# A decoder layer on one core: the causal mask of all scores added by VectorE while it takes the maxima, in place of mask products on TensorE

## The chip, the cores and the metric

The kernel runs as one program on one core of a Trainium2 chip. The metric is the device time of one execution in microseconds, lower is better; of several executions the median counts. The engines are named as in the profile: PE is TensorE (PEld its weight loads), DVE VectorE, ACT ScalarE, POOL GpSimd, SP the engine that only issues DMAs.

## What is computed

A decoder layer for 16 sequences of 256 tokens of 512 features, in float32: causal self attention with rotary positions, cross attention over a context, and a mixture of eight experts. Only self attention bears on the change:

```python
q = (x @ wq).reshape(b, s, N_HEADS, HEAD_DIM).transpose(0, 2, 1, 3)     # 32 heads of 16
k = (x @ wk).reshape(b, s, N_KV_HEADS, HEAD_DIM).transpose(0, 2, 1, 3)  # 8, each for 4 heads
...
scores = jnp.einsum('bhqd,bhkd->bhqk', q, k) / HEAD_DIM ** 0.5
causal = jnp.tril(jnp.ones((s, s), dtype=bool))
scores = jnp.where(causal[None, None], scores, -jnp.inf)
probs = jax.nn.softmax(scores, axis=-1)
out = jnp.einsum('bhqk,bhkd->bhqd', probs, v)
```

The softmax subtracts each row's maximum, which is to be taken over the keys up to the query only.

## The kernel before

The stages run one after the other: constants and weights, projections (`stage_qkv`), `stage_attention`, `stage_cross`, `stage_experts`. The change is in `stage_attention`, in one constant, and in the mask's tile.

Attention works in 32 halves: a half is one sequence with 16 of its 32 heads (four groups of keys, each with four query heads). Scores are computed twice. First, with queries as rows, only to find the maxima (`score`, L750 to L762, and the reductions at L654). The negated maxima go into `nb`, are transposed (`turn_m`), copied, and moved by DMA into a 49th row of the queries `qs`. Two halves later the scores are computed again with keys as rows and the maximum subtracted by that 49th row (`shifted`, L764), ScalarE takes the exponential (L592), GpSimd zeroes what lies above the diagonal (L500), and TensorE multiplies by the values (`values`, L774). This second way is not touched.

A half has 12 pieces of the first kind, s0 to s11, in six pairs p = 0 to 5; the two pieces r = 0, 1 of a pair lie in the two halves of the array's rows and are issued in turns. Each piece fills one PSUM bank of 128 x 512: for p = 0, 1 (first 128 queries) four heads of 128 keys, for p = 2 to 5 (last 128 queries) two heads of 256 keys. The first products overwrite the bank. Then one product for each piece, the bf16 identity times the mask (zero up to the diagonal, -1e30 above), is added onto the blocks on the diagonal: 512 columns for p = 0, 1, and 256 for p = 2 to 5. Its end gives the semaphore `scores`. VectorE waits for it and reduces the whole bank in one instruction to 4 or 2 negated maxima.

The banks are a ring of four (`ring`). 18 results pass through it in a half in the order of `TURNS`: s0, s1, m (the maxima turned), qa, s2, s3, s4, s5, qb, qc, s6, s7, s8, s9, qd, k, s10, s11, where qa to qd and k are transposes of the next half's queries and keys, which ScalarE (qa, qb, qd) and VectorE (qc at L630, k at L635) copy out. `taken` makes TensorE wait until the result four turns earlier has been read: so s2 and s3 wait for the maxima of s0 and s1, s6 for s4, s10 for s8. `score` takes both banks before the first product of a pair.

The order on each engine is written out by hand. TensorE, for each p of `step`: `shifted` of the half two before, `score`, then at p = 0 the maxima turned and qa, at p = 1, 3, 5 a product with values, at p = 2 qb and qc, at p = 4 qd and k. VectorE, for each p: the two pieces, then qc at p = 2, k at p = 4, and once in two halves a reciprocal at p = 5.

Outside attention, `stage_constants` lets GpSimd set the mask (L149, L161) while the weights are loaded.

Of the kernel before, what the change touches and what calls it, by code (L numbers as in the profile page):

```python
# [13 lines left out]
BF16 = mybir.dt.bfloat16  # L14
# [21 lines left out]
ST = SLOTS // P  # L36
EPS = 1e-5
MASKED = -1e30
ONE = 1
CH = 4  # L40

# [7 lines left out]
def wait_apart(eng, sem, value, passed, start=ONE):  # L49

    if not (isinstance(value, int) and value <= 0):
        eng.wait_ge(sem, start + value).then_inc(passed, 1)
# [54 lines left out]
def stage_constants(nc, io, t):  # L107


    with Scope(nc) as s:  # L110
# [34 lines left out]
        @block.gpsimd  # L145
        def _(pool):
            pool.memset(t["ident"][:], 0.0).then_inc(ident_set, 1)
            pool.memset(t["identb"][:], 0.0).then_inc(ident_set, 1)
            pool.memset(t["mask"][:], 0.0).then_inc(mask_set, 1)  # L149
            pool.memset(t["ones"][:], 1.0)  # L150
            pool.memset(t["upper"][:], 1.0).then_inc(mask_set, 1)
            pool.memset(t["avg"][:], 1.0 / P)
            pool.memset(t["half"][:], -0.5)
            pool.memset(t["eps"][:], EPS)
            pool.wait_ge(ident_set, ONE + 2)
            for m in (t["ident"], t["identb"]):
                pool.affine_select(out=m[:], in_=m[:], compare_op=ALU.not_equal, fill=1.0, base=0,
                                   pattern=[[-1, P]], channel_multiplier=1)
            pool.wait_ge(mask_set, ONE + 2)

            pool.affine_select(out=t["mask"][:], in_=t["mask"][:], compare_op=ALU.is_ge, fill=MASKED, base=0,  # L161
                               pattern=[[-1, P]], channel_multiplier=1)

            pool.affine_select(out=t["upper"][:], in_=t["upper"][:], compare_op=ALU.is_gt, fill=0.0, base=0,
                               pattern=[[1, P]], channel_multiplier=-1)
# [203 lines left out]
def stage_attention(nc, io, t):  # L369
# [6 lines left out]
    with Scope(nc) as s:  # L376
# [43 lines left out]
        def bank(e, name):  # L420

            return ring[(2 * e + TURNS.index(name)) % 4]
# [203 lines left out]
        def _(dve):  # L626
# [19 lines left out]
            def step(j, w, q, e):  # L646
                h = 2 * j + e
                for p in range(6):
                    if within(h, 0, HALVES):
                        for r in range(2):  # L650
                            n = 2 * p + r
                            heads, qb = (slice(0, REP), 0) if p < 2 else (slice(p // 2 * 2 - 2, p // 2 * 2), 1)
                            dve.wait_ge(sm["scores"], ONE + PIECES * h + n + 1)
                            dve.tensor_reduce(nb[e][:, r, p % 2, heads, qb],  # L654
                                              bank(e, f"s{n}")[:].rearrange("p (h k) -> p h k", h=heads.stop - heads.start),
                                              AX.X, ALU.max, negate=True).then_inc(sm["maxima"], 1)
                    if p == 2 and within(h + 1, 0, HALVES):
                        keep_q(h + 1, (2 * q + e + 1) % 4, bank(e, "qc"))
                    if p == 4 and within(h + 1, 0, HALVES):
                        keep_k(h + 1, (2 * q + e + 1) % 4, bank(e, "k"))  # L660
                    if e == 1 and p == 5 and within(j - 2, 0, B):
                        dve.wait_ge(sm["den_loaded"], ONE + 16 * (j - 2) + 16)
                        wait_apart(dve, sm["rec_stored"], 16 * (j - 2), passed_dve)
                        dve.reciprocal(rec[:], den[:]).then_inc(sm["den_turned"], 1)
                    if p == 5 and isinstance(h, int) and h == HALVES + 1:
                        first_splits()
# [36 lines left out]
        def _(pe):  # L703
# [45 lines left out]
            def score(j, q, e, p):  # L749
                i = 2 * q + e  # L750
                width = P if p < 2 else S
                heads = range(REP) if p < 2 else range(p // 2 * 2 - 2, p // 2 * 2)
                banks = [taken(2 * j + e, e, f"s{2 * p + r}")[:].rearrange("p (h k) -> p h k", k=width) for r in range(2)]
                for c, n in enumerate(heads):
                    for r in range(2):
                        rows = slice(64 * r, 64 * r + 48)
                        pe.matmul(banks[r][:, c, :], qs[i][rows, p % 2, n, width - P:width],
                                  ks[i][rows, p % 2, 0:width], start=True, stop=False, skip_group_check=True)
                for r in range(2):
                    pe.matmul(banks[r][:, :, width - P:width], t["identb"][:],  # L760
                              t["mask"][:].unsqueeze(1).to_broadcast([P, len(heads), P]), start=False, stop=True,
                              skip_group_check=True).then_inc(sm["scores"], 1)  # L762

            def shifted(h, i, p):  # L764
                kb, qb = BLOCKS[p // 2]
# [1025 lines left out]
def decoder_layer(nc, io):  # L1791
    with Scope(nc) as s:
        t = {}
        t["ident"] = s.sb("ident", [P, P])
        t["identb"] = s.sb("identb", [P, P], BF16)
        t["mask"] = s.sb("mask", [P, P], BF16)
        t["ones"] = s.sb("ones", [P, P])
        t["upper"] = s.sb("upper", [P, P])
        t["avg"] = s.sb("avg", [P, P])
# [106 lines left out]
```

## Time and profile before

| | us |
|---|---|
| median of 3 runs | 2931.71 |
| the runs | 2930.7 to 2936.34 |
| the profiled execution | 2930.81 |
| its span, first to last instruction | 2929.1 |
| PE busy | 2793.4 (95%) |
| DVE busy | 1236.7 (42%) |
| ACT busy | 877.9 (30%) |
| POOL busy | 838.8 (29%) |
| mean granted clock of TensorE, as a share of full | 0.982 |

The page divides the span into 40 slices of 73 us. Attention lies in the slices from 188 to 600 us, where DVE is busy for about seven tenths; the experts, from about 1090 us, are two thirds of the span, and the chain that ended last lies nearly all in them. As the stages follow each other, what attention gains or loses moves the end by as much. A busy time is the sum of the recorded durations; instructions that overlap are pipelined, so it is the starts of consecutive instructions that tell what one costs.

### The profile page before, as it was taken

To read this page: it belongs to the slowest core of one execution; us is meant where nothing else is said; L and a number is where in the kernel's file an instruction comes from. 1 tells how busy PE (TensorE), PEld (TensorE's weight loads), DVE (VectorE), ACT (ScalarE), POOL (GpSimd) and SP (SyncE) were. 2 spreads that over 40 slices of the span, in tenths; PEclk is the share of its full clock that TensorE was granted. 3 is DMA by queue.
4 is the path that set the end of the run, shared out by engine and by line. 5 is a ranking of instruction groups with operands and counts; after the bars stand their busy time and mean duration, and the time that the engine had idled before them with its cause. 6 is when DMAs were issued, how large, how long until landed. Compare 5 with 4: busy or idle time off the path is not lost.

```text
span 2929.1 us, 45881 instructions
## 1 busy us (share of the span) xinstructions
PE 2793.4 (95%) x16150; PEld 2283.9 (78%) x16150; DVE 1236.7 (42%) x2152; ACT 877.9 (30%) x1697; POOL 838.8 (29%) x1306
## 2 busy tenths in 40 slices
PE   6989999988999939999999999999999999999998
PEld 6865555556666529999999999999999999999997
DVE  6756777747888833332232232132133133133111
ACT  1126666641555512221121121122122122122110
POOL 4546776631166641101101111011021021011010
PEclk9999999999999969999999999999999999999999
DMA  3101222242122223221122032032033033022010
GB/s 109 43 1 31 48 45 48 55 92 87 68 84 75 77 83 106 91 86 64 51 92 75 26 108 83 15 109 87 12 108 101 11 100 104 14 90 85 26 47 21
DMA packets 97078, 194.68 MB, mean 66 GB/s; under 512 B 22126, under 2 KB 23758, under 8 KB 96800
## 3 DMA queue, kind: packets, MB, share of 16 engines
q1 hardware_dynamic: 75072, 131.77, 15.1%
q0 software_dynamic: 21856, 60.73, 6.6%
q8 instruction: 116, 1.90, 0.3%
q14 instruction: 34, 0.28, 0.0%
HBM read 148.77 MB, written 38.94 MB: 64 GB/s over the span
## 4 chain that ended last, share of the span: by engine, by line
PE 62%; DMA 0%; POOL 0%; DVE 0%; issue 0%; ACT 0%; DVEq 0%; POOLq 0%
PE ex_hid L1775 31%; PE ex_acc L102 10%; PE ex_acc L103 10%; PE ex_acc L104 10%; PE ex_xb L1745 1%; DMA ex_ys<-xn_dram,ex_slot_gather 0%; POOL out_dram L1627 0%; POOL ex_ys L1607 0%; DVE ex_ys L1688 0%; POOL ex_xg L1592 0%; DMA ex_ys<-slot_table_dram 0%; PE ex_acc L1745 0%; DVE ex_h0l L1696 0%; ACT ex_h0h L1655 0%; DVE ex_xT0l L1671 0%
## 5 line engine op out<-in xcount | busy, mean ns | idle before, releaser
L1696 DVE SCALAR_TENSOR_TENSOR ex_h0l<-ex_hid,ex_h0h 128x640 fp32r<-128x640 f32 x128 | 105.5, 824 | 682.8 <-ACT ex_h0h L1655 682.8
L1696 DVE SCALAR_TENSOR_TENSOR ex_h1l<-ex_hid,ex_h1h 128x640 fp32r<-128x640 f32 x128 | 105.4, 824 | 602.9 <-ACT ex_h1h L1655 602.3
L1655 ACT ACTIVATE ex_h0h<-ex_hid 128x640 fp32r<-128x640 f32 x128 | 90.1, 704 | 734.5 <-PE ex_hid L1775 734.5
L1655 ACT ACTIVATE ex_h1h<-ex_hid 128x640 fp32r<-128x640 f32 x128 | 90.1, 704 | 729.8 <-PE ex_hid L1775 729.8
L654 DVE TENSOR_REDUCE at_nb<-at_ring 128x2 f32<-128x512 f32 (+1 forms) x384 | 246.8, 685 | 121.1 <-PE at_ring L760 120.9
L1597 POOL COPY ex_gi<-ex_slot_gather 128x1 int32 (+1 forms) x82 | 15.3, 187 | 918.2 <-PE ex_xb L1745 913.3
L102 PE MATMUL ex_acc<-ex_w_h,ex_h1h 128*128 128x512 f32 x640 | 254.8, 398 | 0.0
L102 PE MATMUL ex_acc<-ex_w_h,ex_h0h 128*128 128x512 f32 x640 | 253.4, 396 | 0.0
L103 PE MATMUL ex_acc<-ex_w_l,ex_h0h 128*128 128x512 f32 x640 | 250.3, 391 | 0.0
L103 PE MATMUL ex_acc<-ex_w_l,ex_h1h 128*128 128x512 f32 x640 | 250.2, 391 | 0.0
L104 PE MATMUL ex_acc<-ex_w_h,ex_h1l 128*128 128x512 f32 x640 | 249.8, 390 | 0.0
L104 PE MATMUL ex_acc<-ex_w_h,ex_h0l 128*128 128x512 f32 x640 | 249.5, 390 | 0.0
L592 ACT ACTIVATE at_pT<-at_st 128x512 f32<-128x512 f32 x384 | 210.4, 609 | 124.1 <-PE at_st L770 124.1
L1775 PE MATMUL ex_hid<-ex_xT0h,ex_w_h 128*128 128x320 f32 x1024 | 234.3, 310 | 3.4 <-DVE ex_xT0l L1671 1.4
L1775 PE MATMUL ex_hid<-ex_xT0h,ex_w_l 128*128 128x320 f32 x1024 | 234.2, 310 | 0.0
L1775 PE MATMUL ex_hid<-ex_xT0l,ex_w_h 128*128 128x320 f32 x1024 | 234.1, 310 | 0.0
L1775 PE MATMUL ex_hid<-ex_xT1h,ex_w_l 128*128 128x320 f32 x1024 | 233.4, 309 | 0.0
L1775 PE MATMUL ex_hid<-ex_xT1l,ex_w_h 128*128 128x320 f32 x1024 | 233.3, 309 | 0.0
L1775 PE MATMUL ex_hid<-ex_xT1h,ex_w_h 128*128 128x320 f32 x1024 | 232.7, 308 | 0.0
L1627 POOL DMA_INDIRECT out_dram<-ex_ys,ex_rows_out x80 | 80.7, 1009 | 519.5 <-DVE ex_ys L1688 504.9
L1775 PEld LDWEIGHTS ex_hid<-ex_xT0h,ex_w_h 128*128 128x128 f32 x1024 | 176.7, 189 | 15.4 <-issue 4.1
L1775 PEld LDWEIGHTS ex_hid<-ex_xT1h,ex_w_h 128*128 128x128 f32 x1024 | 176.4, 188 | 10.0
(273 smaller groups left out, 5665.2 us busy)
## 6 DMA issues: line engine op xcount, KB each, us to landing
ex_raw<-in_w_tiles_dram SPq DMA_DIRECT2D x256, 256.0 KB, 2.8
x_in<-in_x_dram SPq DMA_DIRECT2D x32, 256.0 KB, 2.7
act<-at_raw SPq DMA_DIRECT2D x128, 64.0 KB
at_recb<-o_rec_dram SPq DMA_DIRECT2D x16, 512.0 KB
k<-in_x_dram SPq DMA_DIRECT2D x32, 256.0 KB, 2.7
cx_ctx<-in_ctx_dram SPq DMA_DIRECT2D x16, 512.0 KB, 3.8
out_dram<-cx_res SPq DMA_DIRECT2D x16, 512.0 KB, 2.8
xn_dram<-cx_prob SPq DMA_DIRECT2D x16, 512.0 KB, 2.8
```

The source lines that it names most:

```text
L102: eng.matmul(out, lhs[0], rhs[0], start=first, stop=False, **kw)
L103: eng.matmul(out, lhs[0], rhs[1], start=False, stop=False, **kw)
L104: return eng.matmul(out, lhs[1], rhs[0], start=False, stop=last, **kw)
L592: act.activation(pT[slot][:], st[n % 3][:], ACT.Exp).then_inc(sm["probs"], 1)
L654: dve.tensor_reduce(nb[e][:, r, p % 2, heads, qb], bank(e, f"s{n}")[:].rearrange("p (h k) -> p h k", h=heads.stop - heads.start), AX.X, AL ...
L1597: pool.tensor_copy(gi[r][:], slot_gather[:, bass.ds(n, 1)]).then_inc(sm["idx_col"], 1)
L1627: pool.indirect_dma_start(io["out_rows"][:, :], bass.IndirectOffsetOnAxis(rows_out[:, i:i + 1], 0), ys[:, i, :], None, bounds_check=B * S ...
L1655: act.activation(h[f % 2][0][:], hid[:, :, 0:HB], ACT.Relu).then_inc(sm["h_hi"], 1)
L1696: dve.scalar_tensor_tensor(h[f % 2][1][:], hid[:, :, 0:HB], 0.0, f32(h[f % 2][0][:]), ALU.max, ALU.subtract).then_inc(sm["h_lo"], 1)
L1745: q = pe.transpose(bank[:, k * P:(k + 1) * P], source[:, k * P:(k + 1) * P], t["ident"][:])
L1775: i = pe.matmul(hid[:, z, 0:HB], w1[a][:, f, k, :], xT[b][q][:, k, z * HB:(z + 1) * HB], start=k == 0 and a + q == 0, stop=k == KD - 1 and ...
```

## The change

The products with the mask are taken out, and the last score product of a piece gives the semaphore. The mask's tile is 256 columns wide, the first 128 of them zero, so that it fits a head of 256 keys; the last 128 fit a head of 128. VectorE takes a piece head by head: an operation adds the mask to the head's scores, multiplies by -1, writes the result back over the scores, and puts the smallest of the results, which is the negated maximum, into `nb`. Its wait is an instruction of its own.

```diff
+LARGEST = 3e38
...
-            pool.affine_select(out=t["mask"][:], in_=t["mask"][:], compare_op=ALU.is_ge, fill=MASKED, base=0,
+            pool.affine_select(out=t["mask"][:, P:S], in_=t["mask"][:, P:S], compare_op=ALU.is_ge, fill=MASKED, base=0,
                                pattern=[[-1, P]], channel_multiplier=1)
...
                             n = 2 * p + r
-                            heads, qb = (slice(0, REP), 0) if p < 2 else (slice(p // 2 * 2 - 2, p // 2 * 2), 1)
-                            dve.wait_ge(sm["scores"], ONE + PIECES * h + n + 1)
-                            dve.tensor_reduce(nb[e][:, r, p % 2, heads, qb],
-                                              bank(e, f"s{n}")[:].rearrange("p (h k) -> p h k", h=heads.stop - heads.start),
-                                              AX.X, ALU.max, negate=True).then_inc(sm["maxima"], 1)
+                            x = bank(e, f"s{n}")
+                            wait_apart(dve, sm["scores"], PIECES * h + n + 1, passed_dve)
+                            width, qb, heads = (P, 0, range(REP)) if p < 2 else (S, 1, range(p // 2 * 2 - 2, p // 2 * 2))
+                            for c, a in enumerate(heads):
+                                y = x[:, c * width:c * width + width]
+                                m = dve.tensor_tensor_reduce(y, y,
+                                                             t["mask"][:, S - width:S], -1.0, LARGEST, ALU.add, ALU.min,
+                                                             nb[e][:, r, p % 2, a, qb:qb + 1])
+                            m.then_inc(sm["maxima"], 1)
...
-                        pe.matmul(banks[r][:, c, :], qs[i][rows, p % 2, n, width - P:width],
-                                  ks[i][rows, p % 2, 0:width], start=True, stop=False, skip_group_check=True)
-                for r in range(2):
-                    pe.matmul(banks[r][:, :, width - P:width], t["identb"][:],
-                              t["mask"][:].unsqueeze(1).to_broadcast([P, len(heads), P]), start=False, stop=True,
-                              skip_group_check=True).then_inc(sm["scores"], 1)
+                        m = pe.matmul(banks[r][:, c, :], qs[i][rows, p % 2, n, width - P:width],
+                                      ks[i][rows, p % 2, 0:width], start=True, stop=True, skip_group_check=True)
+                        if c == len(heads) - 1:
+                            m.then_inc(sm["scores"], 1)
...
-        t["mask"] = s.sb("mask", [P, P], BF16)
+        t["mask"] = s.sb("mask", [P, S], BF16)
```

## Rows read from the trace of the kernel before

**Rows 1.** Windows: stretch, then busy us (x instructions) by engine, granted clock, DMA.
```profile
400.00:450.00 50.00, 49.24 (x394) 26.99 (x390) 35.22 (x57) 34.09 (x70) 36.92 (x54) 1.00 0.21 43
```
**Rows 2.** Waits from 250 to 550 us: who waited for whom, total us, times, longest.
```profile
DVE at_nb L654 <- PE at_ring L760: 87.8, 139, 1.2
...
PEld at_ring L757 <- DVE at_nb L654: 25.7, 70, 0.6
```
**Rows 3.** Timeline, PE: start, us, line, operation, out<-in, count [idle before].
```profile
456.84 0.60 PE L760 MATMUL at_ring<-mask,identb 128*128 128x512 bf16 x2
457.28 0.27 PE L746 MATMUL at_ring<-ident,at_nb 128*32 128x128 f32 x1
...
458.61 0.66 PE L757 MATMUL at_ring<-at_ks,at_qs 48*128 48x128 f32 x8 [0.19 <-DVE at_nb L654]
459.20 0.60 PE L760 MATMUL at_ring<-mask,identb 128*128 128x512 bf16 x2
459.74 1.07 PE L784 MATMUL at_pv<-at_pT,at_vc 128*32 128x512 f32 x8
460.74 0.50 PE L770 MATMUL at_st<-at_qs,at_ks 49*128 49x512 f32 x2
461.07 0.40 PE L757 MATMUL at_ring<-at_ks,at_qs 48*128 48x256 f32 x4
461.41 0.39 PE L760 MATMUL at_ring<-mask,identb 128*128 128x256 bf16 x2
461.64 1.04 PE L727 MATMUL at_ring<-ident,at_qst 128*128 128x128 f32 x8
```
**Rows 4.** Timeline of the same half on DVE.
```profile
457.27 1.29 DVE L654 TENSOR_REDUCE at_nb<-at_ring 128x4 f32<-128x512 f32 x2 [0.96 <-PE at_ring L760]
459.63 1.29 DVE L654 TENSOR_REDUCE at_nb<-at_ring 128x4 f32<-128x512 f32 x2 [1.07 <-PE at_ring L760]
461.73 1.29 DVE L654 TENSOR_REDUCE at_nb<-at_ring 128x2 f32<-128x512 f32 x2 [0.81 <-PE at_ring L760]
...
463.83 1.29 DVE L654 TENSOR_REDUCE at_nb<-at_ring 128x2 f32<-128x512 f32 x2 [0.22 <-PE at_ring L760]
465.82 1.29 DVE L654 TENSOR_REDUCE at_nb<-at_ring 128x2 f32<-128x512 f32 x2 [0.70 <-PE at_ring L760]
...
469.12 0.54 DVE L664 RECIPROCAL at_rec<-at_den 128x64 f32<-128x64 f32 x1
470.17 1.29 DVE L654 TENSOR_REDUCE at_nb<-at_ring 128x4 f32<-128x512 f32 x2 [0.50 <-PE at_ring L760]
```
**Rows 5.** Timeline, DVE: the first maxima of halves 0, 3 and 31.
```profile
189.43 1.29 DVE L654 TENSOR_REDUCE at_nb<-at_ring 128x4 f32<-128x512 f32 x2 [1.23 <-PE at_ring L760]
...
224.20 1.29 DVE L654 TENSOR_REDUCE at_nb<-at_ring 128x4 f32<-128x512 f32 x2 [0.96 <-PE at_ring L760]
...
587.66 1.29 DVE L654 TENSOR_REDUCE at_nb<-at_ring 128x4 f32<-128x512 f32 x2 [0.97 <-PE at_ring L760]
```
**Rows 6.** Timeline, DVE in cross attention: 512 and 1024 columns.
```profile
1003.90 0.69 DVE L1214 TENSOR_REDUCE cx_nmx<-cx_bank 128x1 f32<-128x512 f32 x1
1004.51 1.22 DVE L1233 TENSOR_TENSOR cx_res<-cx_ctx,act 128x1024 f32<-128x1024 f32 x1
```
**Rows 7.** Timeline, ACT in cross attention: operations with an accumulator output.
```profile
1004.83 0.68 ACT L1135 ACTIVATE cx_prob<-cx_bank,cx_nmx 128x512 f32<-128x512 f32 x1
1005.40 0.20 ACT L1135 ACTIVATION_READ_ACCUMULATOR cx_prob<-cx_bank,cx_nmx 128x1 f32 x1
1005.49 0.69 ACT L1135 ACTIVATE cx_prob<-cx_bank,cx_nmx 128x512 f32<-128x512 f32 x1
```
**Rows 8.** Timeline, DVE in cross attention: two tiny instructions in a row.
```profile
1009.67 0.25 DVE L1315 BATCH_NORM_AGGREGATE cx_mv<-cx_st 128x2 f32<-128x6 f32 x2
```
**Rows 9.** Timeline, DVE behind attention: the second has a wait instruction ahead of it.
```profile
652.19 0.68 DVE L670 TENSOR_TENSOR at_qs<-act,at_qs 128x512 fp32r<-128x512 f32 x1
...
652.79 0.69 DVE L682 BATCH_NORM_STATS2 op_st<-act 128x6 f32 x1
```

## The prediction

> **What bounds the kernel now.** I read the slices of the page first. Attention (0.19 to 0.60 ms of the span) is the only stage the change touches; before it lie the projections, behind it cross attention and the experts, whose instructions stay as they are. The stretch 400 to 450 us [rows 1] shows TensorE busy for 49.2 of 50 us at the full clock, VectorE for 35.2. A busy TensorE is not TensorE at its peak, so I went on to the waits [rows 2]: from 250 to 550 us VectorE waits 87.8 us for the mask products, and TensorE's weight loads of the scores wait 25.7 us for the maxima. The two pass the four ring banks back and forth. Then I laid one half (12 pieces) of TensorE [rows 3] beside the same half of VectorE [rows 4]. The half begins at 457.27 and the next at 470.17: 12.90 us. The first maxima of half 3 start at 224.20 and of half 31 at 587.66 [rows 5], so the mean of 28 halves is 12.98 us.
>
> In that half two things alternate. After s0 and s1, TensorE has to wait for both banks (s2 and s3 take the banks of s0 and s1): VectorE ends at 458.56, the eight products of s2 and s3 start at 458.61, their masks at 459.20, and VectorE starts again at 459.63, idle for 1.07 us. From there to s8 TensorE's own list is the later one: values 1.00 us (459.74 to 460.74), shifted scores 0.33 (to 461.07), scores 0.34, masks 0.23 (to 461.64), transposes. VectorE waits 0.81, 0.22 and 0.70 us for it. So both matter, TensorE more.
>
> **What the change takes away.** A half has two pairs of mask products of 512 columns, 0.44 us a pair (456.84 to 457.28), and four of 256 columns, 0.23 us a pair (461.41 to 461.64) [rows 3]: 2 x 0.44 + 4 x 0.23 = 1.80 us, in 32 halves 57.6 us of TensorE. That is the most it could give, and only if nobody else becomes late. It also shortens every answer to VectorE by one mask product: the maxima can start when the last score is out.
>
> **What it adds on VectorE.** Now a piece is one reduction over 512 columns; two in a row last 1.29 us, one of them 0.685, so the pitch is 0.605 us [rows 4]. The slope of a column comes from 1024 columns in 1.22 us against 512 in 0.69 [rows 6]: 1.04 ns. Of the 0.605 us, 0.532 are columns and 0.073 is the fixed part of an instruction. After the change pieces 0 to 3 are four operations over 128 columns each, pieces 4 to 11 two over 256: the columns stay the same, the fixed part is paid 32 times a half, not 12 times. One operation is 0.133 + 0.073 = 0.206 us, or 0.266 + 0.073 = 0.339 us.
>
> These operations also put out an accumulator, and no VectorE row does that. The nearest rows are ScalarE's [rows 7]: its exponential with a sum is an ACTIVATE and, 0.57 us later, a row of its own, ACTIVATION_READ_ACCUMULATOR, after which the next ACTIVATE starts 0.09 us later. I expect the same pair on VectorE. The price of the read is bounded below by nothing (the read lies wholly beside the next operation) and above by two amounts: the read waits until the main operation is through (its full 0.152 us of latency, 0.685 - 0.533, not 0.073) and then takes its own slot. Between them stands the pitch of two tiny VectorE instructions, 0.25 us for two of 0.165, so 0.085 us [rows 8]; ScalarE's 0.09 agrees. I take 0.085: a pair costs 0.291 us (128) or 0.424 us (256). A piece then costs 1.16 us (0 to 3) or 0.85 us (4 to 11) in place of 0.605. VectorE's work of a half grows from 14 x 0.605 + 0.22 (half a reciprocal) = 8.7 us to 4 x 1.16 + 8 x 0.85 + 2 x 0.605 + 0.22 = 12.9 us, by itself as long as the half is now.
>
> The Trainium skill, "Vector Engine (DVE) Microarchitecture Reference", section 5.2, gives about 75 ns of fixed cost per instruction, and "VectorE: DVE Perf Modes", section "Two Vector instructions with no wait between them", says that an operation with an accumulator output is two instructions. The trace agrees with the first (0.073 and 0.085) and shows the second for ScalarE alone. By 75 ns for each of the two a half would be 0.3 us shorter than mine and the whole some 8 us faster. Against this change speaks a rule of "VectorE: DVE Perf Modes", section "Rules for kernel authors": it is the number of VectorE operations that is to be kept small, not that of semaphores.
>
> Two smaller costs. Each piece now waits in an instruction of its own. Where the signal is there already that costs nothing: 652.19 to 652.79 is a plain 0.60 us over such a wait [rows 9]. Where VectorE really waits (three times a half), I put 0.05 us, between 0 and 0.1; only the next maxima are queued behind it, and TensorE waits for those. Writing the scores back in place (PSUM to PSUM) has no row either; I take it at nothing, since the write goes beside the reading, and its upper end is half the rate. The larger mask is set once by GpSimd while the projections' weights are still loading, with 180 us to go before its first use; at nothing.
>
> **The half afterwards, laid out in time** (us from the first maxima of the half). s0, s1: 8 x 0.291 = 2.33. Then TensorE must wait for both banks: 0.08 until the last result is out, 0.05 to TensorE, 0.66 for eight score products, 0.05 back, 0.05 for the wait: 3.22. s2, s3 to 5.55. Meanwhile TensorE does values, shifted, s4 and s5 (1.00 + 0.33 + 0.5) and is ready at about 4.9. s4, s5: 4 x 0.424 to 7.25. One copy of queries to 7.85. s6 and s7 need the bank of s5: TensorE from 7.38, out 7.88, VectorE from 7.98 to 9.68. For s8 TensorE is ready at 9.60 (7.82 + 1.00 + 0.33 + 0.45), so on to 11.38. The keys' copy to 11.98, s10 and s11 from 12.11 to 13.81. The next s0 is ready at 14.00; every other half the reciprocal (0.45) ends later, at 14.26. Mean 14.13 us against 12.98: TensorE's list has fallen behind VectorE's everywhere but at the bank waits, and its 1.80 us lie idle.
>
> **The sum.** 28 halves x 1.15 = 32.2 us. The first three halves have little or no value work beside them; now they take 224.20 - 189.43 = 34.8 us [rows 5], then 3 x 13.86 = 41.6: 6.8 more. The last, without copies, goes from 12.2 to about 13.7: 1.5 more. Together 40.5 us. The profiled run took 2930.81 us (span 2929.1), 0.9 under the median of 2931.71, so nothing is to be corrected: 2930.8 + 40.5 = 2971 us, 1.4% slower.
>
> **Rivals.**
> The accumulator's read costs nothing, or is no instruction (faster). Pairs cost 0.206 and 0.339 us, a piece 0.82 or 0.68. VectorE's work is 10.1 us, s2 starts at 2.5, and from there TensorE's list without masks decides: s4 4.2, s6 6.2, s8 7.9, s10 10.0, next s0 11.8. That is 1.18 us less a half: 28 x 1.18 and about 1 more, 2897 us. For it: the waits on the mask products [rows 2] go. Against it: the ScalarE rows. Between 11.8 at no cost and 14.13 at 85 ns, the break-even of 12.98 lies at a read of 43 ns. Chance 0.14.
> The read lands near that point, gain and loss cancel, 2931 +- 6 us. Chance 0.05.
> The read waits for the end of the main operation: 0.418 + 0.085 = 0.503 and 0.370 us a pair, 32 x 0.079 = 2.5 us a half more, of which 0.1 falls into idle time: 32 x 2.4 = 77 us on top, 3048 us. For it: a result must be complete before it is read. Against: ScalarE's read starts 0.12 us before its ACTIVATE's recorded end (0.68 long, read after 0.57). Chance 0.15.
> In-place PSUM traffic halves the rate: 16 x 0.266 + 16 x 0.133 = 6.4 us a half, 3175 us; nothing in the trace for or against. Chance 0.04.
> TensorE, idle in more places, is granted the lower of its two clocks in attention (1.2 instead of 2.4 GHz): its 9.6 us of a half (values 3 x 1.00, transposes 5 x 0.44 + 0.11, shifted 6 x 0.33, scores 4 x 0.33 + 2 x 0.49, from [rows 3]) double and the half is about 19 us, 3165 us. The row of 400 to 450 shows 1.00 although the engine waits inside it, and the gaps that come are under 1.5 us. Chance 0.02.
>
> **How the numbers follow.** The forecast, a VectorE-bound half of 13.4 to 15.0 us, has 0.60 and by itself 2945 to 3005 us (read at 60 to 120 ns, waits 0 to 0.1). Adding the case of no change (down to 2925) and that of the late read (up to 3055) leaves 0.20 out: range 2925 to 3055. A measurement of this kernel tells about 0.2%, 6 us, from no change. Faster 0.14; within 0.2% 0.05; slower 0.60 + 0.15 + 0.04 + 0.02 = 0.81.
>
> **What the profile after would show.** Attention some 40 us longer, everything behind it moved and nothing else changed. VectorE's share in 400 to 450 us from 35 to about 46 of 50 us. 1024 rows of the new operation with 1024 reads of the accumulator, main rows about 0.42 and 0.28 us long, starts 0.42 and 0.29 us apart. VectorE's idle time almost all before s2; TensorE's weight loads of scores waiting for the maxima for well over 100 us in all. No mask products, granted clock 1.00. The forecast is wrong if no read rows appear, if their pitch is far from 0.085, or if the pitch of the main operation isn't that of its columns.

## The result and the profile after

The changed kernel takes 2993.81 us in the median of 4 runs (2989.59 to 2998.31), the kernel before 2932.74; the ratio of the runs is 1.0207, interval 1.0194 to 1.022. It is 61 us slower. The forecast was 2971 us, 40 slower, in a range of 2925 to 3055: the sign and the range were right, the size was short by 21 us. The profiled execution took 2998.31 us (span 2996.6, against 2929.1 before: 67.5 more).

The page of the changed kernel: the busy times, and the clock granted to TensorE in 40 slices of 75 us.

```profile
PE 2793.0 (93%) x15766; PEld 2288.9 (76%) x15766; DVE 1329.6 (44%) x3816; ACT 879.1 (29%) x1697; POOL 844.8 (28%) x1306
...
PEclk9979888888999997999999999999999999999999
...
q14 instruction: 62, 0.51, 0.1%
```

Two things stand in it that the prediction did not have. The clock is at eight tenths in the slices 5 to 10 (300 to 749 us) and at seven in the third, where the kernel before has nine tenths or more in each; and TensorE is busy for 2793 us as before (2793.4), although 57.6 us of products are gone: the rest runs slower. One of the two queues that bring instructions (q14) moved 62 packets in place of 34.

The stretch that answers to [rows 1] (busy us and instructions of PE, PEld, DVE, ACT, POOL, then granted clock), and the waits that answer to [rows 2]:

```profile
400.00:450.00 50.00, 43.83 (x327) 24.10 (x327) 43.39 (x234) 32.78 (x67) 32.10 (x47) 0.93 0.19 36
450.00:500.00 50.00, 41.17 (x276) 22.70 (x274) 37.55 (x210) 28.06 (x58) 27.48 (x42) 0.83 0.20 42
```
```profile
PEld at_ring L762 <- DVE at_nb L658: 64.4, 52, 5.0
PE at_ring L762 <- DVE at_nb L658: 48.4, 49, 4.7
...
DVE at_ring L658 <- PE at_ring L762: 43.6, 81, 1.4
...
DVE at_ring L658 <- issue: 13.2, 8, 2.2
```

TensorE now waits longer for the maxima, 64.4 us at its weight loads where it was 25.7 (the second row is for the most part the same waits, seen at the products), and VectorE half as long for TensorE (43.6 where it was 87.8). The last row is new: VectorE stood still 8 times, 1.2 to 2.2 us each, for nothing that the profile shows. The groups of operations from 250 to 550 us (count, busy us, mean ns):

```profile
L658 DVE CUSTOM_DVE_ANT_0 at_ring<-at_ring,mask 128x256 f32<-128x256 f32 x320 | 126.7, 458 | 21.2 <-PE at_ring L762 20.5
L658 DVE DVE_READ_ACCUMULATOR2_ANT at_nb<- 128x1 f32 x643 | 91.5, 142 | 0.0
L658 DVE CUSTOM_DVE_ANT_0 at_ring<-at_ring,mask 128x128 f32<-128x128 f32 x323 | 82.5, 327 | 36.4 <-PE at_ring L762 23.2 <-issue 13.2
```

The accumulator's read is a row of its own, one for each operation. What it costs is told by the starts. VectorE's timeline (start, duration):

```profile
440.41 0.34 DVE L658 CUSTOM_DVE_ANT_0 at_ring<-at_ring,mask 128x128 f32<-128x128 f32 x1
440.66 0.14 DVE L658 DVE_READ_ACCUMULATOR2_ANT at_nb<- 128x1 f32 x1
440.66 0.34 DVE L658 CUSTOM_DVE_ANT_0 at_ring<-at_ring,mask 128x128 f32<-128x128 f32 x1
...
442.29 0.47 DVE L658 CUSTOM_DVE_ANT_0 at_ring<-at_ring,mask 128x256 f32<-128x256 f32 x1
442.67 0.15 DVE L658 DVE_READ_ACCUMULATOR2_ANT at_nb<- 128x1 f32 x1
442.67 0.47 DVE L658 CUSTOM_DVE_ANT_0 at_ring<-at_ring,mask 128x256 f32<-128x256 f32 x1
```

Operations over 128 columns start 0.25 us apart, those over 256 0.38. The read is recorded over the start of the next operation, so adding its 142 ns to the others would count it twice. From 440.16 to 441.90 lie seven steps, from 441.90 to 443.43 four, so the pitches are 249 and 382 ns: 43 ns over the 206 and 339 that the prediction gave the main operation, half of the 85 it gave the read.

Now a turn of VectorE's loop. Attention has a rolled loop of five bodies of four halves, so four turns; this is the third, VectorE and then TensorE:

```profile
449.86 0.55 DVE L669 RECIPROCAL at_rec<-at_den 128x64 f32<-128x64 f32 x1
452.52 0.30 DVE L658 CUSTOM_DVE_ANT_0 at_ring<-at_ring,mask 128x128 f32<-128x128 f32 x1 [2.11 <-issue]
...
454.79 0.30 DVE L658 CUSTOM_DVE_ANT_0 at_ring<-at_ring,mask 128x128 f32<-128x128 f32 x1 [1.17 <-issue]
```
```profile
450.82 0.49 PE L773 MATMUL at_st<-at_qs,at_ks 49*128 49x512 f32 x2
455.95 1.12 PE L762 MATMUL at_ring<-at_ks,at_qs 48*128 48x128 f32 x8 [4.64 <-DVE at_nb L658]
457.00 1.93 PE L787 MATMUL at_pv<-at_pT,at_vc 128*32 128x512 f32 x8
```

VectorE stops for 2.11 and 1.17 us, TensorE therefore idles for 4.64 us, and then does its eight products with the values in 1.93 us, where they took 1.07 [rows 3]: its clock has fallen to the lower level (granted 0.50 from 456 to 462 us). The other turns look the same (2.15 and 1.14 us, 2.14 and 1.16, 2.08 and 1.27).

### The profile page after: what moved, and what is told of

Read it like the earlier page. It is cut to its first block, busy times and chain, and to the rows that moved or that the text cites. A ratio compares the mean times of both kernels' runs of the same rounds, so it can differ in the third digit from the quotient of the medians.

```text
span 2996.6 us, 47161 instructions
## 1 busy us (share of the span) xinstructions
PE 2793.0 (93%) x15766; PEld 2288.9 (76%) x15766; DVE 1329.6 (44%) x3816; ACT 879.1 (29%) x1697; POOL 844.8 (28%) x1306
## 4 chain that ended last, share of the span: by engine, by line
PE 61%; DMA 0%; POOL 0%; issue 0%; DVE 0%; DVEq 0%; ACT 0%; POOLq 0%
PE ex_hid L1778 30%; PE ex_acc L104 10%; PE ex_acc L103 10%; PE ex_acc L105 10%; PE ex_xb L1748 1%; DMA ex_ys<-xn_dram,ex_slot_gather 0%; POOL out_dram L1630 0%; POOL ex_ys L1610 0%; DVE ex_ys L1691 0%; POOL ex_xg L1595 0%; DMA ex_ys<-slot_table_dram 0%; PE ex_acc L1748 0%; DVE ex_xT0l L1674 0%; DVEq L73 0%; ACT ex_xT0h L1641 0%
## 5 line engine op out<-in xcount | busy, mean ns | idle before, releaser
L658 DVE CUSTOM_DVE_ANT_0 at_ring<-at_ring,mask 128x256 f32<-128x256 f32 (+1 forms) x1024 | 331.8, 393 | 92.9 <-PE at_ring L762 78.6
L501 POOL TENSOR_SCALAR_AFFINE_SELECT at_pT<-at_pT 128x512 f32<-128x512 f32 x256 | 154.9, 635 | 112.1 <-ACT at_pT L593 112.1
```

The source lines that it names most:

```text
L501: pool.affine_select(out=x[:], in_=x[:], compare_op=ALU.is_ge, fill=0.0, base=0, pattern=[[0, REP], [1, P]], channel_multiplier=-1).then_i ...
L658: m = dve.tensor_tensor_reduce(y, y, t["mask"][:, S - width:S], -1.0, LARGEST, ALU.add, ALU.min, nb[e][:, r, p % 2, a, qb:qb + 1])
```

## The experiments

Each kernel's time is given against the kernel before on the same chip. A half is measured from one copy of keys on VectorE to the next; undisturbed means at full clock and away from a turn. It is 12.90 us before and 13.24 to 13.50 us in the changed kernel.

**e1_after_unrolled: the changed kernel with VectorE's loop written out.**

```diff
+        def steps(eng, first, step, unroll=False):
...
+                for j in range(19):
+                    for e in range(2):
+                        step(j, j // 2, j % 2, e)
...
-            steps(dve, first, step)
+            steps(dve, first, step, unroll=True)
```

> The changed kernel, but VectorE's 38 half steps of attention are written out one by one, where five turns of a loop covered 20 of them. In the changed kernel's trace VectorE stands still for 2.1 and 1.15 us, with no releaser, at each of the four points where that loop turns, TensorE then waits 4.6 us, and its granted clock falls. Theory A (three causes: VectorE's longer work, some 0.5 us a half, 16 us; the loop's turns, because the body has become about 380 instructions long; the clock that falls after the gaps): the eight stops vanish, the clock rises in part, 2970 us, 2960 to 2980. Rival B (the stops belong to the new operation, not to the loop): they stay in place and the time stays at 2990 to 2998 us.

Measured: 2971.17 us (2965.17 to 2980.21) against 2929.21, ratio 1.0152 (1.0126 to 1.0177), so +42 where the changed kernel has +61. All eight stops named "issue" are gone. What is left at full clock is this start of s2, TensorE and VectorE:

```profile
521.00 0.50 PE L778 MATMUL at_st<-at_qs,at_ks 49*128 49x512 f32 x2
522.63 0.66 PE L767 MATMUL at_ring<-at_ks,at_qs 48*128 48x128 f32 x8 [1.13 <-DVE at_nb L663]
```
```profile
523.48 0.30 DVE L663 CUSTOM_DVE_ANT_0 at_ring<-at_ring,mask 128x128 f32<-128x128 f32 x1 [0.90 <-PE at_ring L767]
```

The products end at 523.29, the maxima start at 523.48. In two of four 50 us stretches from 350 to 550 us the clock is still 0.90 (e9 and the three runs behind it take that up).

**e2_before_long_body: the kernel before, with 256 waits that are satisfied already, spread over VectorE's loop body.** Its body has then about as many instructions as the changed one (some 378; before, some 122).

```diff
+            def fill(h, p):
+                if not isinstance(h, int):
+                    for _ in range(6 if p % 3 == 0 else 5):
+                        wait_apart(dve, sm["filled"], 5, passed_dve)
...
+                            fill(h, p)
```

> The kernel before, with 256 waits that are long fulfilled put behind the reductions in VectorE's loop body, so that the body has as many instructions as in the changed kernel (about 380); no operation of the change is in it. Theory A: VectorE stands still for 2 to 3 us at the four turns of the loop, and the time rises by 12 us for these and more where the clock falls: 2945 to 2965 us. Rival B: no stops, at most a few us for the waits themselves: 2931 to 2938 us.

Measured: 2955.31 us (2954.62 to 2956.73), ratio 1.009 (1.0073 to 1.0107), +26. The same stops come at the same four places, 2.54, 2.78, 2.46 and 2.47 us:

```profile
315.08 0.55 DVE L670 RECIPROCAL at_rec<-at_den 128x64 f32<-128x64 f32 x1 [0.19 <-issue]
318.17 1.48 DVE L659 TENSOR_REDUCE at_nb<-at_ring 128x4 f32<-128x512 f32 x2 [2.54 <-issue]
```

About 17 of the 26 us lie in the four halves with a stop (16.73 to 18.35 us each, against 13.14 beside them). The satisfied waits cost a little by themselves: the other 16 halves of the loop take 13.12 to 13.27 us and not 12.90, some 4 us in all.

**e13_before_unrolled: the kernel before, written out in the same way.**

> The kernel before, with the loop over pairs of heads written out instead of rolled, and nothing else. Theory A (a loop body that is too long for what VectorE keeps is what pays at a turn, and before's body is short enough): nothing changes, 2928 to 2935 us. The rival (unrolling gains by itself, so that the 22 us that it gave the changed kernel say nothing of the change): 2920 us or less.

Measured: 2931.37 us (2929.87 to 2933.6, 10 runs) against 2932.0, ratio 0.9999 (0.999 to 1.0009). So it is not the loop that costs but its length: a body of some 122 instructions turns for nothing, one of some 378 stops. The instruction queue's packets go the same way (34 before, 56 in e2, 62 after, 51 in e1). The Trainium skill, "Advanced Engine Details and Errata", section "ISA Cache", says that an engine other than TensorE keeps two lines of 256 instructions; the runs agree in so far as a body of 378 pays and one of 122 doesn't, and none lies between. By that size two lines hold 512 instructions, so it doesn't say by itself that 378 must pay. That it is the fetching of the body's start that stops VectorE is inferred from this and the packets; the profile only says "issue".

**e3_dve_part_alone and e4_pe_part_alone: the two parts apart.** e3 has VectorE's new operations and keeps the mask products; e4 has no mask products and keeps the reduction of a whole bank, so its maxima run over all keys of a piece.

```diff
-                for r in range(2):
-                    pe.matmul(banks[r][:, :, width - P:width], t["identb"][:],
-                              t["mask"][:].unsqueeze(1).to_broadcast([P, len(heads), P]), start=False, stop=True,
-                              skip_group_check=True).then_inc(sm["scores"], 1)
```

> VectorE's part alone: maxima head by head with the mask added as in the changed kernel, and TensorE's mask products kept (the mask is added twice, which changes nothing). TensorE has 1.8 us more work a half than in the changed kernel, and VectorE waits one mask product longer at the bank waits. Theory A (TensorE's clock falls because it has too little to do): the clock comes back to near 1.00, and with more work the kernel is faster than the changed one: about 2975 us. Rival C (the clock has little to do with it; the halves are as long as VectorE makes them): slower than the changed kernel by 5 to 15 us: 3000 to 3010 us.

Measured: 3037.86 us (3034.11 to 3038.55), ratio 1.0366 (1.0349 to 1.0383), +109: slower than either theory had it. An undisturbed half is 14.86 us, 1.5 to 1.6 more than in the changed kernel. VectorE's timeline shows why (from s2 on, the last number the idle time before):

```profile
302.79 0.30 DVE L658 CUSTOM_DVE_ANT_0 at_ring<-at_ring,mask 128x128 f32<-128x128 f32 x1 [1.23 <-PE at_ring L765]
307.50 0.43 DVE L658 CUSTOM_DVE_ANT_0 at_ring<-at_ring,mask 128x256 f32<-128x256 f32 x1 [0.42 <-PE at_ring L765]
309.49 0.43 DVE L658 CUSTOM_DVE_ANT_0 at_ring<-at_ring,mask 128x256 f32<-128x256 f32 x1 [0.35 <-PE at_ring L765]
312.08 0.43 DVE L658 CUSTOM_DVE_ANT_0 at_ring<-at_ring,mask 128x256 f32<-128x256 f32 x1 [0.42 <-PE at_ring L765]
```

With VectorE the later engine, each bank goes back late, and every way back carries a mask product. So taking them away is worth 44 to 48 us beside the slow VectorE as well (3038 to 2994), and the prediction's "its 1.80 us lie idle" was wrong.

> TensorE's part alone: no mask products, and VectorE takes the maxima with one reduction a piece as before, now over all keys, masked ones too. This leaves the mask of the maxima out; the softmax is the same for any subtracted value that keeps the exponentials in range. Laid out in time as in the prediction a half is about 11.1 us against 12.98: 1.9 us less, 60 us in all, 2872 us, as long as the clock stays at 1.00. If the clock falls here too (theory D: every relief of TensorE is paid back by its clock) 2900 us or more. If the mask products were hidden anyway: 2925 us or more.

Measured: 2876.17 us (2873.16 to 2878.02), ratio 0.9817 (0.9801 to 0.9833): 53 us faster than the kernel before, 114 faster than the changed one (-53 against +61). From 250 to 550 us a half is 10.94 to 11.23 us, the clock full:

```profile
400.00:450.00 50.00, 48.53 (x411) 27.36 (x410) 41.09 (x66) 39.53 (x83) 42.98 (x66) 1.00 0.26 52
```
```profile
446.16 1.29 DVE L654 TENSOR_REDUCE at_nb<-at_ring 128x4 f32<-128x512 f32 x2 [0.54 <-PE at_ring L757]
448.20 1.29 DVE L654 TENSOR_REDUCE at_nb<-at_ring 128x4 f32<-128x512 f32 x2 [0.75 <-PE at_ring L757]
...
457.13 1.29 DVE L654 TENSOR_REDUCE at_nb<-at_ring 128x4 f32<-128x512 f32 x2
```

This is the best kernel of the study, and it computes the same result: a softmax is the same whatever is subtracted, as long as the exponentials stay in range, and what lies above the diagonal is zeroed behind the exponential anyway. What it gives up is that range: were a masked score far above all the others of its row, they would vanish. With this case's inputs they don't. The two parts nearly add up: +109 - 53 = +56 against +61 measured together, a difference within the intervals.

**e9_plain_wait: e1 with the wait carried by the first operation of a piece.**

```diff
-                            wait_apart(dve, sm["scores"], PIECES * h + n + 1, passed_dve)
+                            dve.wait_ge(sm["scores"], ONE + PIECES * h + n + 1)
```

> As e1, but the wait for the scores is carried by the operation, as in the kernel before, not by an instruction of its own. If that instruction delays each blocked start by 0.15 us (theory W): the starts come 0.04 us after the score products' end, at four to five such places a half 0.5 us less, 2971 - 16 = 2955 us. If the new operation starts late by itself (theory O): 0.19 us as before and 2971 us.

Measured: 2969.65 us (2967.47 to 2971.74), ratio 1.0128 (1.0111 to 1.0145), +38 against +42: nearly no change. But the undisturbed half did fall, to 12.78 to 12.91 us. TensorE and VectorE at the start of s2:

```profile
442.58 0.50 PE L778 MATMUL at_st<-at_qs,at_ks 49*128 49x512 f32 x2
444.22 0.66 PE L767 MATMUL at_ring<-at_ks,at_qs 48*128 48x128 f32 x8 [1.13 <-DVE at_nb L663]
444.81 1.93 PE L792 MATMUL at_pv<-at_pT,at_vc 128*32 128x512 f32 x8
```
```profile
444.91 0.30 DVE L663 CUSTOM_DVE_ANT_0 at_ring<-at_ring,mask 128x128 f32<-128x128 f32 x1 [0.75 <-PE at_ring L767]
```

The maxima start 0.69 us after the products do; in e1 it was 0.85. The 0.16 us are the wait's. In this very half the clock falls: the values take 1.93 us (granted 0.50 from 445 us), with no turn near. The granted clock of the eight stretches from 200 to 600 us is 0.67 0.78 0.94 0.90 0.90 0.90 0.86 0.97 (e1: 0.72 0.93 1.00 0.90 1.00 0.90 0.99 1.00). What the wait gave, more falls of the clock took.

**e5_more_shifted_work, e16_still_more_work, e15_plain_wait_more_work: more products where TensorE waits.** If it is idle time that lets the clock fall, useless work in it must make the kernel faster. The shifted products, which overwrite their bank and so can be repeated, stand just before the waits for the banks.

```diff
-                    pe.matmul(st[n % 3][:], ks[i][rows, p % 2, kb * P:kb * P + P],
-                              qs[i][rows, p % 2, :, qb * P:qb * P + P], start=True, stop=True)\
-                        .then_inc(sm["shifted"], 1)
+                    for _ in range({1: 4, 3: 2, 5: 2}.get(p, 1)):
+                        m = pe.matmul(st[n % 3][:], ks[i][rows, p % 2, kb * P:kb * P + P],
+                                      qs[i][rows, p % 2, :, qb * P:qb * P + P], start=True, stop=True)
+                    m.then_inc(sm["shifted"], 1)
```

e5 is e1 with each of p = 1, 3, 5 twice; e16 is e1 with 4, 3, 3 times; e15 is e9 with 4, 2, 2 times (the diff).

> The changed kernel with VectorE's steps written out (as e1), and TensorE's shifted-score products of p = 1, 3 and 5 issued twice, the second over the first with the same result. They stand right in front of the bank waits, where TensorE idles 0.45 to 1.1 us, and take 0.33 us a pair. So they should lie in idle time and only make TensorE's gaps shorter. Theory A (TensorE's clock falls for want of work, and the halves in which it falls are 0.5 to 2 us longer): the clock stays higher than in e1 in attention, and the kernel with more work is as fast or faster, 2958 to 2968 us against e1's 2971. Rival (the long halves have another cause): 2971 us or up to 5 us more, with the same long halves.

> The unrolled kernel with its own waiting instruction, with the shifted products of the first part given four times and those of the second and third three times. Theory A (work in TensorE's gaps holds its clock): fewer stretches below 1.00 than with each doubled, undisturbed halves still of 13.24 us, and 2952 to 2960 us. The rival (the doubled products had done all that such work can): 2963 us or more.

> The unrolled kernel with the wait carried by the operation, with the shifted products of the first part given four times and those of the second and third twice, where TensorE waits anyway. Theory A (the clock falls because TensorE idles between score blocks, and work in those gaps holds it): the granted clock is near 1.00 in most stretches of the attention, the undisturbed half stays at 12.8 to 13.0 us, and the time falls to 2940 to 2950 us. The rival (the clock follows something else, or the products cost what they fill): 2970 us or more.

Measured: e5 2963.02 us (2961.54 to 2964.25), ratio 1.0108 (1.0091 to 1.0125), as expected by theory A. e16 2961.82 us (2956.86 to 2966.92), ratio 1.0103 (1.0086 to 1.012), which lies between its two expectations and can't be told from e5. e15 2946.66 us (2944.16 to 2947.93), ratio 1.005 (1.0033 to 1.0067), as expected. The stretch from 400 to 450 us of e9 and of e15:

```profile
400.00:450.00 50.00, 43.90 (x328) 24.17 (x320) 43.41 (x247) 31.61 (x66) 35.25 (x51) 0.90 0.20 41
```
```profile
400.00:450.00 50.00, 47.54 (x388) 26.71 (x386) 46.16 (x262) 34.84 (x71) 36.15 (x53) 1.00 0.23 48
```

and TensorE before s2 in e15, which idles 0.44 us where it was 1.13:

```profile
452.65 1.20 PE L779 MATMUL at_st<-at_qs,at_ks 49*128 49x512 f32 x8
454.29 0.66 PE L767 MATMUL at_ring<-at_ks,at_qs 48*128 48x128 f32 x8 [0.44 <-DVE at_nb L663]
```

640 more instructions on TensorE (320 products, each with its weight load) make e9 23 us faster (e9 +38, e15 +15). The longest wait of the score products for the maxima from 250 to 550 us is 1.4 us in e1, 1.1 in e9 and e5 (which has three stretches left at 0.93), 0.6 in e16 and 0.4 in e15. All six stretches from 250 to 550 us stand at 1.00, in e16 too, and nearly every half takes 12.78 to 12.90 us in e15 (13.23 to 13.36 in e16, apart from a few up to 13.7). e16 is 15 us above e15: with the clock held in both, that is the price of the waiting instruction, 0.45 us a half. (e16 has 128 products more as well; but the undisturbed halves of e1 and e9, which have none added, differ by the same 0.45.)

**e7_before_more_shifted_work: the kernel before with p = 1, 3, 5 twice.** It asks what the mask products were covered by.

> The same doubled products in the kernel before. There TensorE's own list decides from s2 to s8, and it idles only 0.2 us before s2; so of 3 x 0.33 us a half 0.7 to 0.9 should count, in 32 halves 22 to 29 us: 2952 to 2958 us. If TensorE has slack in the kernel before (mask products hidden anyway) it stays within 2929 to 2936 us.

Measured: 2930.36 us (2928.06 to 2933.18, 10 runs), ratio 0.9996 (0.9986 to 1.0006): nothing, where 20 us and more had been expected. TensorE in it, and one row of the kernel before:

```profile
458.24 0.73 PE L771 MATMUL at_st<-at_qs,at_ks 49*128 49x512 f32 x4
458.93 0.66 PE L757 MATMUL at_ring<-at_ks,at_qs 48*128 48x128 f32 x8
```
```profile
463.07 0.51 PE L757 MATMUL at_ring<-at_ks,at_qs 48*128 48x256 f32 x4
```

The pair doubled takes 0.73 us where it took 0.50, and each of the three stands before a bank wait: before s2 TensorE idled for 0.19 us in the kernel before [rows 3], and its products of s6 and s7 start at 463.07, when the maxima of s5 have just ended (461.73 + 1.29 = 463.02 [rows 4]). So TensorE's own list decides only between these places. The prediction has that for s2, but it counted s6 to TensorE's list ("from there to s8"), and there the reading was wrong.

**e8_reduced_by_head and e14_by_head_plain_wait: heads without mask and accumulator.** e8 is e1 with a plain reduction for each head, so again maxima over all keys; e14 also gives up the waiting instruction.

```diff
-                                m = dve.tensor_tensor_reduce(y, y,
-                                                             t["mask"][:, S - width:S], -1.0, LARGEST, ALU.add, ALU.min,
-                                                             nb[e][:, r, p % 2, a, qb:qb + 1])
+                                m = dve.tensor_reduce(nb[e][:, r, p % 2, a, qb:qb + 1], y, AX.X, ALU.max,
+                                                      negate=True)
```

> As e1, but VectorE takes each head's maximum with a plain reduction: 32 operations a half without accumulator reads; there is no mask in the maxima (left out, over all keys, as in e4). The trace of the changed kernel has pitches of 0.249 (128 columns) and 0.382 us (256), which are 0.206 and 0.339 by the fixed part of an instruction plus 0.043 for the read. Theory A: the pitches here are 0.206 and 0.339 us, the half about 11.8 us, the whole 2892 to 2905 us. Rival (an operation on one head costs more than its columns and 0.073 us, and the read is free): the pitches stay 0.249 and 0.382, 2960 us or more. It also tells where the late start after a wait comes from: in e1 the first operation begins 0.19 us after the recorded end of the last score product, in e4 0.04. If the wait in an instruction of its own does it, it is 0.19 here too and the time is up to 20 us above that; if the new operation does it, 0.04.

Measured: 2923.55 us (2918.02 to 2926.33, 8 runs), ratio 0.9973 (0.9962 to 0.9984). The rows, TensorE and VectorE:

```profile
439.15 0.66 PE L766 MATMUL at_ring<-at_ks,at_qs 48*128 48x128 f32 x8 [0.79 <-DVE at_nb L663]
...
451.07 0.66 PE L766 MATMUL at_ring<-at_ks,at_qs 48*128 48x128 f32 x8 [0.80 <-DVE at_nb L663]
```
```profile
439.95 3.08 DVE L663 TENSOR_REDUCE at_nb<-at_ring 128x1 f32<-128x128 f32 x12 [0.86 <-PE at_ring L766]
...
449.34 1.68 DVE L663 TENSOR_REDUCE at_nb<-at_ring 128x1 f32<-128x128 f32 x8 [0.40 <-PE at_ring L766]
452.23 3.00 DVE L663 TENSOR_REDUCE at_nb<-at_ring 128x1 f32<-128x128 f32 x12 [1.21 <-PE at_ring L766]
...
455.93 1.42 DVE L663 TENSOR_REDUCE at_nb<-at_ring 128x1 f32<-128x256 f32 x4
```

Eight reductions last 1.68 us and one 0.28, so the pitch is (1.68 - 0.28) / 7 = 0.200 us; of the wide ones (1.42 - 0.42) / 3 = 0.333 us. These are the prediction's 0.206 and 0.339, and the half of 11.93 us is near its 11.8. The total is 19 to 32 us above the forecast: the clock is 0.70 and 0.79 from 550 to 650 us, and s2 starts late. The products of s2 end at 439.81 and its maxima start at 439.95, 0.14 us later, and so it is in nearly every half. The half with 451.73 and 452.23, 0.50 us, is the only one from 250 to 550 us with such a start, and it is 0.28 us longer than the others (12.21).

> The run that reduced by head (no mask, plain reductions, one a head), now with the wait carried by the reduction itself instead of standing in an instruction of its own. If both late starts of that run (0.50 us at s2, 0.22 us at the others) come of the waiting instruction, its half of 11.93 us falls to about 11.1; if only the 0.22 us does, to about 11.4; if neither, it stays at 11.93. If the granted clock stays where it was, the time falls below 2900 us with either of the first two; if it falls further, as it did when the wait was taken into the masked operation, the time stays near 2920 us.

Measured: 2904.69 us (2899.7 to 2905.67) against 2932.0, ratio 0.9909 (0.9892 to 0.9925), 19 us less than e8. A half falls to 11.59 to 11.61 us, which is none of the three figures expected. The late start is gone:

```profile
463.02 0.66 PE L766 MATMUL at_ring<-at_ks,at_qs 48*128 48x128 f32 x8 [0.68 <-DVE at_nb L663]
```
```profile
463.71 3.08 DVE L663 TENSOR_REDUCE at_nb<-at_ring 128x1 f32<-128x128 f32 x12 [0.75 <-PE at_ring L766]
```

The products end at 463.68, the maxima start at 463.71. From the start of the products of s2 to their maxima it is 0.69 us, in e8 0.80 (439.15 to 439.95), so the waiting instruction costs 0.11 us here; three of them are the 0.33 us of the half. The expectation of 11.1 us took the 0.50 us of one odd half for the rule. In 32 halves 0.33 us are 11 of the 19 us; the rest goes with the clock, 0.83 and 1.00 from 550 to 650 us. What delayed that one start stays open.

## Why the prediction was right, and where not

The total was forecast well, and partly by luck: the range of 2925 to 3055 held, but half of the 61 us (turns of the loop and falls of the clock) has causes that the prediction's sum doesn't hold, while its own largest term didn't come. The 61 us can be laid out by runs (medians, each over the kernel before of its chip):

| kernel | over before | step | us |
|---|---|---|---|
| changed | +61 | turns of a long loop body | 19 |
| e1, written out | +42 | falls of the clock inside attention | 12 |
| e16, clock held | +30 | the waiting instruction | 15 |
| e15, its wait in the operation | +15 | heads, mask and accumulator against the mask products saved | 15 |

A step is the difference of two medians, and by the intervals (57 to 65, 37 to 52, 25 to 35 and 10 to 20 us over before) each is known to some 5 to 9 us only. The first is also known from the other side: 17 of the 26 us in e2. In e15 the last maxima end 10.6 us later than before (610.52 against 599.88), and 9 of these arise in the first three halves (42.3 us between the copies of keys of the first four halves, against 33.5). From there on a half is as long as before. Behind attention another 7 us come, where the clock is 0.50 for 40 us (600 to 640) and was low for some 14 before; up to the end 2 to 3 of them are made up again (span 2944.0 against 2929.1).

Point by point:

- Which engine decides. VectorE became the later one, as forecast: it is busy for 46.2 of 50 us where nothing disturbs it (e15; forecast about 46, in the changed kernel 37.6 to 43.4). But its undisturbed half is 13.24 to 13.50 us, at or below the lower end of the forecast 13.4 to 15.0. Two of the marks were off. The weight loads wait 64.4 us and not "well over 100", since the maxima took less than laid out. And VectorE's idle time is not almost all before s2: 23.2 us lie before the pieces of 128 columns and 20.5 before those of 256, the latter from the waiting instruction and from TensorE at the lower clock; in e15, with neither, it is 19.8 and 3.5 us.
- What is taken away. The mask products are worth 57.6 us by the rows, and e4 shows 53. The prediction called that the most it could give. In the steady half it gave more than the 1.80 us of the rows, 12.90 to 10.95, since the maxima also start sooner; the first three halves took 2 us more in place of less.
- The main operation. 0.206 and 0.339 us, from the slope of [rows 6] and the fixed part of [rows 4], were measured as 0.200 and 0.333 (e8). Writing back in place costs nothing to be seen.
- The accumulator's read. It is an instruction of its own, as in [rows 7], but costs 43 ns and not 85. This is the term of the sum that was mis-sized most, and by the prediction's own sign of being wrong ("if their pitch is far from 0.085") this step failed: two tiny instructions of [rows 8] were the wrong neighbour, as were ScalarE's [rows 7]. "Main rows about 0.42 and 0.28 us long" did not hold either (0.458 and 0.327), nor did the pitches 0.424 and 0.291 (0.382 and 0.249).
- The layout of the half. It holds well. Between its two ends, 11.8 us at no cost and 14.13 at 85 ns, lies 12.98 at 43 ns, of which 0.15 at most are for three waits; without these 12.83 to 12.98, and e15 measures 12.78 to 12.90. The rival "the read lands near that point, gain and loss cancel" with its chance of 0.05 described the steady half; it did not describe the kernel.
- The waiting instruction. Put at 0.05 us where VectorE really waits, it costs 0.16 us at s2 (e1 against e9), and 0.45 us a half (13.24 to 13.34 against 12.78 to 12.91 undisturbed), 15 us in all. [Rows 9] showed one that was satisfied and could bear on nothing else. The step "between 0 and 0.1" was too narrow.
- The turns. Not in the prediction at all. It counted each added instruction's time but not where they stand: 256 more instructions in a rolled body. 19 us.
- The clock. The rival was priced as all or nothing (19 us a half, 3165 us, chance 0.02; 32 halves of 19 us would give about 3125), with "the gaps that come are under 1.5 us" against it. It came in part: the gaps stayed under 1.5 us away from the turns, as said, and still the clock fell in some halves, which then took 0.6 to 2.2 us more (13.85 to 15.41 us in e1); forecast was 1.00, the stretches from 250 to 550 us show 0.81 to 0.93. A rival with two ends only leaves out the case that happened. In e9 the clock is seen to fall behind a gap of 1.13 us; in e1 a gap of the same length left it at full, and the runs don't show what tells the two apart. That idle time of TensorE is the cause is shown by e15 against e9 and by e16 against e1, where nothing else was changed.
- The first and last halves. 6.8 us were forecast for the first three, 9 measured in e15, with the clock at 0.50 until about 225 us (before, until about 198). Either part does that by itself: in e4 it is 0.50 until about 223 us, in e3 again 0.50 from 210 to 225.

So the total came out near the forecast for partly other reasons. Of the sum of 40.5 us some 32 didn't come (28 halves of 1.15 us, since the read costs 43 ns), and some 52 came that were not in it: turns 19, clock 12, waits 15 (the 4 that stood in the sum are among the 32), the first halves 2, behind attention 4 to 5. 40.5 - 32 + 52 is 60.5, against 61. The break-even of 43 ns was met in the steady half, and the kernel lost all the same.

The rivals: that the read waits for the end of the main operation, and that PSUM traffic halves the rate, are both excluded by the pitches of 0.249 and 0.382 us.

## What to carry to other kernels

Splitting one long VectorE instruction into many costs the fixed part of each (73 ns here), about 49 ns more for an accumulator output and a second operand (0.249 against 0.200 us, 0.382 against 0.333), and the place they take in a rolled loop: count the instructions of the body, and write the loop out if it grows past what turned for nothing before. Here an added wait of TensorE was paid twice, once in time and once in its clock, so look at the granted clock before you move work off TensorE. And before moving a mask to another engine, ask whether the result needs it there at all: leaving it out of the maxima (e4) gave 53 us where moving it lost 61.

## What the runs showed of the hardware that was not expected

- Useless products made a kernel faster: e15 has 640 TensorE instructions more than e9 (47106 in the profile against 46466) and takes 23 us less, as the granted clock in the stretches from 250 to 550 us rises from 0.78 to 0.94 to a plain 1.00.
- A pair of shifted products (one in each half of the array's rows) repeated at once lasts 0.23 us longer (0.50 to 0.73).
- A wait in an instruction of its own, when it really blocks, starts its successor about 0.16 us later than a wait that the operation carries (0.85 against 0.69 us after the products' start), and 0.11 us later before a plain reduction (0.80 against 0.69).
- VectorE stops for 2.1 and 1.2 us, or once for 2.5 to 2.8 us, at each turn of a loop body of some 378 instructions, and not at all at 122.
- An accumulator read of 142 ns recorded moves the next start by 43 to 49 ns only.
